# One graph-attention kernel: the queue orders of the last pair of heads are written out by hand

## The reference

```
h = relu(layernorm(x))
q = h @ wq.T + bq ; k, v likewise                    # 1024 x 1024 each
q2 = (q @ wiq.T + biq) as 16 heads of 64 ; k2, v2 likewise
mask = 384 x 384, -inf except at the 6,528 edges, where it is softplus(weight of the edge's type)
scores = q2 @ k2.T / 8 + mask ; attn = softmax(scores) ; o = attn @ v2   # for each head
out = x + (o of all heads, 384 x 1024) @ wo.T + bo
```

## Time and profile before

| | us |
|---|---|
| median of 3 runs | 301.51 |
| the runs | 300.0, 301.51, 301.77 |
| the profiled execution | 299.9 |
| its span, first to last instruction | 298.2 |
| PE busy | 286.0 |
| DVE, ACT, POOL busy | 179.3, 159.4, 153.4 |
| mean granted clock of PE | 0.994 |

### The profile page before, as it was taken

One profiled execution on the slowest core, in us unless ns is written; L12 is line 12 of the kernel. 1 busy time (PEld: TensorE's weight loads), 2 busy tenths in 40 slices (PEclk: granted clock), 3 DMA queues, 4 the chain that ended last, 5 costly groups with the idle time before them and its releaser, 6 DMA issues. The chain is left out here.

```text
span 298.2 us, 5957 instructions
## 1 busy us (share of the span) xinstructions
PE 286.0 (96%) x2325; PEld 266.7 (89%) x2325; DVE 179.3 (60%) x442; ACT 159.4 (53%) x287; POOL 153.4 (51%) x157
## 2 busy tenths in 40 slices
PE   6999999999999999999999899999999998959996
PEld 3799998888999999999999899999999995748885
DVE  4999778697576434444468665757666565372131
ACT  3886234362465223444345788778787879362000
POOL 6452445454465565554015959485674949660000
PEclk9999999999999999999999999999999999799999
DMA  7977865727634444344974234050421214200031
GB/s 264 326 248 269 311 212 189 228 75 261 244 129 143 141 143 141 96 116 113 261 178 106 63 82 120 25 141 20 126 73 70 86 61 141 73 0 2 0 141 70
DMA packets 16078, 40.90 MB, mean 137 GB/s; under 512 B 3737, under 2 KB 5170, under 8 KB 16050
## 3 DMA queue, kind: packets, MB, share of 16 engines
q1 hardware_dynamic: 13602, 38.53, 40.9%
q0 software_dynamic: 2016, 1.21, 1.8%
q10 hardware_dynamic: 432, 0.79, 0.7%
HBM read 37.71 MB, written 2.81 MB: 136 GB/s over the span
## 5 line engine op out<-in xcount | busy, mean ns | idle before, releaser
L483 POOL DMA_INDIRECT cells<-value,cell x51 | 55.3, 1085 | 56.2 <-DMA cells<-value,cell 40.5
L530 ACT ACTIVATE w_hi<-raw 128x1024 fp32r<-128x1024 f32 x50 | 51.7, 1054 | 22.8 <-PE banks L947 19.1
L945 PE MATMUL banks<-a_hi,w_hi 128*128 128x384 f32 x184 | 61.5, 334 | 0.0
L947 PE MATMUL banks<-a_lo,w_hi 128*128 128x384 f32 x184 | 61.5, 334 | 0.0
L946 PE MATMUL banks<-a_hi,w_lo 128*128 128x384 f32 x184 | 61.5, 334 | 0.0
L456 POOL TENSOR_TENSOR w_lo<-raw,w_hi 128x1024 fp32r<-128x1024 f32 x15 | 36.0, 2406 | 37.8 <-ACT w_hi L530 37.8
L817 DVE TENSOR_TENSOR w_lo<-raw,w_hi 128x1024 fp32r<-128x1024 f32 x35 | 42.3, 1229 | 9.9 <-ACT w_hi L530 9.8
L945 PEld LDWEIGHTS banks<-a_hi,w_hi 128*128 128x128 f32 x184 | 34.5, 188 | 0.1
L946 PEld LDWEIGHTS banks<-a_hi,w_lo 128*128 128x128 f32 x184 | 34.5, 188 | 0.0
L947 PEld LDWEIGHTS banks<-a_lo,w_hi 128*128 128x128 f32 x184 | 34.5, 188 | 0.0
L642 ACT ACTIVATE prob<-prob,neg_max 128x384 f32<-128x384 f32 x48 | 29.1, 607 | 9.1 <-DVE neg_max L877 9.0
(11 more groups left out here) (146 smaller groups left out, 600.3 us busy)
## 6 DMA issues: line engine op xcount, KB each, us to landing
raw<-in_slabs SPq DMA_DIRECT2D x40, 512.0 KB, 3.6
raw<-in_slabs SPq DMA_DIRECT2D x32, 256.0 KB, 3.9
prob<-key_rows SPq DMA_DIRECT2D x8, 256.0 KB, 4.2
x_sb<-in_x SPq DMA_DIRECT2D x3, 512.0 KB, 5.9
out_y<-x_sb SPq DMA_DIRECT2D x5, 256.0 KB, 2.1
cells<-prob SPq DMA_DIRECT2D x2, 576.0 KB, 7.6
cells<-value,cell POOLq DMA_INDIRECT x51, 3.4
x_sb<-in_x ACTq DMA_DIRECT2D x3, 256.0 KB, 4.2
```

The lines of the kernel that those rows point to most:

```text
L483: nc.gpsimd.indirect_dma_start(out=cells[c][:, :], out_offset=bass.IndirectOffsetOnAxis(ap=cell[:, t:t + 1], axis=0), in_=value[:, t:t + 1 ...
L530: nc.scalar.activation(split_place(s)[0], raw_place(s), ACT.Copy).then_inc(slab_hi, 1)
L945: nc.tensor.matmul(psum, w[0], a[0], start=first, stop=False)
L947: return nc.tensor.matmul(psum, w[0], a[1], start=False, stop=last)
```

## The change

On ACT, DVE and POOL the loop over pairs ends one pair earlier, and the last pair gets its own list. On ACT the exponentials of pair 7 and the `pt_hi` parts of pair 6 go ahead of the splitting of slabs 51 to 55. On DVE `head_part(5)` goes behind two maxima of pair 7, and the `pt_lo` and `head_part` calls of pairs 6 and 7 are dealt anew. On POOL the scaling of pair 7 comes ahead of all five slabs, with `pair_lo_part(5)` inside it. On PE the output products between the attention steps of the last pair are grouped anew: block 5 of pieces 0 and 1 joins one visit, and block 6 of pieces 0, 1 and 2 goes behind `pair_values(7)`. Away from the last pair there are two edits: on PE four of the 48 steps of pair 2 go ahead of `scores(1, 0)`, and on DVE `y_part(2)` goes behind the two `tile_lo_part` of pair 1.

```diff
--- before.py
+++ after.py
@@ -66,8 +66,9 @@
 LO_ALL = QK0 + 2 + AHEAD
 
 
-SLABS_OF_STEP = [((37 + 2 * j,), (38 + 2 * j,)) for j in range(PAIRS - 1)] + [((51, 52), (53,)), ((54, 55), ())]
-assert [s for step in SLABS_OF_STEP for part in step for s in part] == list(range(LO_ALL, SLABS))
+SLABS_OF_STEP = [((37 + 2 * j,), (38 + 2 * j,)) for j in range(PAIRS - 1)]
+LAST_SLABS = [51, 52, 53, 54, 55]
+assert [s for step in SLABS_OF_STEP for part in step for s in part] + LAST_SLABS == list(range(LO_ALL, SLABS))
 
 
 def tiles_of(group):
@@ -509,17 +510,24 @@
                     nc.gpsimd.tensor_scalar(prob_chunk(j, n, x), prob_chunk(j, n, x),
                                             row_inv[:, j % 2, c:c + 1], 1.0, ALU.mult, ALU.mult).then_inc(prob_ok, 1)
 
-            for j in range(PAIRS + 1):
+            for j in range(PAIRS - 1):
                 first, second = SLABS_OF_STEP[j]
-                if 2 <= j < PAIRS:
+                if j >= 2:
                     pair_lo_part(j - 2)
                 for s in first:
                     split_lo(s)
-                if j < PAIRS:
-                    for n in range(NT):
-                        norm_part(j, n)
+                for n in range(NT):
+                    norm_part(j, n)
                 for s in second:
                     split_lo(s)
+
+            last = PAIRS - 1
+            norm_part(last, 0)
+            norm_part(last, 1)
+            pair_lo_part(last - 2)
+            norm_part(last, 2)
+            for s in LAST_SLABS:
+                split_lo(s)
 
         @block.scalar
         def _(act):
@@ -661,30 +669,43 @@
                     nc.scalar.activation(half_sum[own, :], head_bank[x][other, 0:N], ACT.Identity,
                                          bias=bias[own, b:b + 1]).then_inc(half_ok, 1)
 
-            for j in range(PAIRS + 1):
+            for j in range(PAIRS - 1):
                 first, second = SLABS_OF_STEP[j]
-                if 2 <= j < PAIRS:
+                if j >= 2:
                     pair_hi_part(j - 2)
                 for s in first:
                     split_hi(s)
-                if j < PAIRS:
-                    for n in range(NT):
-                        exp_part(j, n)
+                for n in range(NT):
+                    exp_part(j, n)
                 if j >= 1:
-                    for m in range(2):
+                    for m in range(NT):
                         pt_hi_part(j - 1, m)
-                if j == PAIRS:
-                    pair_hi_part(PAIRS - 2)
-                if j >= 1:
-                    pt_hi_part(j - 1, 2)
-                if j < PAIRS - 1:
-                    for second_of in range(2):
-                        tile_hi_part(3 * KT + 2 * (j + 1) + second_of)
+                for second_of in range(2):
+                    tile_hi_part(3 * KT + 2 * (j + 1) + second_of)
                 for s in second:
                     split_hi(s)
                 if j >= 1:
                     half_part(j - 1)
-            pair_hi_part(PAIRS - 1)
+
+            last = PAIRS - 1
+            exp_part(last, 0)
+            exp_part(last, 1)
+            pt_hi_part(last - 1, 0)
+            pair_hi_part(last - 2)
+            exp_part(last, 2)
+            pt_hi_part(last - 1, 1)
+            pt_hi_part(last - 1, 2)
+            for s in LAST_SLABS[0:3]:
+                split_hi(s)
+            pt_hi_part(last, 0)
+            pt_hi_part(last, 1)
+            half_part(last - 1)
+            pt_hi_part(last, 2)
+            pair_hi_part(last - 1)
+            split_hi(LAST_SLABS[3])
+            half_part(last)
+            pair_hi_part(last)
+            split_hi(LAST_SLABS[4])
 
         @block.vector
         def _(dve):
@@ -906,33 +927,45 @@
                 dve.wait_ge(y_in, 16 * (NT + 1))
                 nc.vector.tensor_tensor(y[:, t, :], y[:, t, :], bo_sb, ALU.add).then_inc(y_ok, 1)
 
-            for j in range(PAIRS + 1):
-                if j < PAIRS:
-                    max_part(j, 0)
-                    if j == 0:
-                        y_part(0)
-                    max_part(j, 1)
-                    inv_part(j, 0)
-                    if j == 0:
-                        y_part(1)
-                    max_part(j, 2)
-                    inv_part(j, 1)
-                    if j == 0:
-                        y_part(2)
-                    inv_part(j, 2)
+            for j in range(PAIRS - 1):
+                max_part(j, 0)
+                if j == 0:
+                    y_part(0)
+                max_part(j, 1)
+                inv_part(j, 0)
+                if j == 0:
+                    y_part(1)
+                max_part(j, 2)
+                inv_part(j, 1)
+                inv_part(j, 2)
                 if j >= 1:
-                    for m in range(2):
+                    for m in range(NT):
                         pt_lo_part(j - 1, m)
-                if j == PAIRS:
-                    pair_lo_part(PAIRS - 2)
-                if j >= 1:
-                    pt_lo_part(j - 1, 2)
-                if j < PAIRS - 1:
-                    for second_of in range(2):
-                        tile_lo_part(3 * KT + 2 * (j + 1) + second_of)
-                if j >= 1:
+                for second_of in range(2):
+                    tile_lo_part(3 * KT + 2 * (j + 1) + second_of)
+                if j == 0:
+                    y_part(2)
+                if 1 <= j < PAIRS - 2:
                     head_part(j - 1)
-            pair_lo_part(PAIRS - 1)
+
+            last = PAIRS - 1
+            max_part(last, 0)
+            max_part(last, 1)
+            inv_part(last, 0)
+            head_part(last - 2)
+            inv_part(last, 1)
+            max_part(last, 2)
+            pt_lo_part(last - 1, 0)
+            inv_part(last, 2)
+            pt_lo_part(last - 1, 1)
+            pt_lo_part(last - 1, 2)
+            pt_lo_part(last, 0)
+            pt_lo_part(last, 1)
+            head_part(last - 1)
+            pt_lo_part(last, 2)
+            pair_lo_part(last - 1)
+            head_part(last)
+            pair_lo_part(last)
             dve.wait_ge(y_ok, NT)
             for i, (_, n, cols_out, psum) in enumerate(out_pieces):
                 dve.wait_ge(out_done, i + 1)
@@ -1153,12 +1186,12 @@
             pair_steps(1, 30, 40)
             scores(0, 2)
             pair_steps(1, 40, 48)
-            pair_steps(2, 0, 8)
+            pair_steps(2, 0, 12)
             for j in range(1, PAIRS - 1):
                 scores(j, 0)
-                pair_steps(j + 1, 8, 16)
+                pair_steps(j + 1, 12 if j == 1 else 8, 18 if j == 1 else 16)
                 scores(j, 1)
-                pair_steps(j + 1, 16, 24)
+                pair_steps(j + 1, 18 if j == 1 else 16, 24)
                 scores(j, 2)
                 pair_steps(j + 1, 24, 32)
                 turn(j - 1, 0)
@@ -1186,16 +1219,14 @@
             pair_values(last - 1)
             turn(last, 0)
             turn(last, 1)
-            out_part(1, range(3, 5))
-            for n in range(2):
-                out_part(n, range(5, 6))
+            out_part(1, range(3, 6))
+            out_part(0, [5])
             turn(last, 2)
-            for n in range(2):
-                out_part(n, range(6, 7))
             pair_values(last)
 
-
-            out_part(2, range(0, 7))
+            out_part(2, range(0, 6))
+            for n in range(3):
+                out_part(n, [6])
             out_part(3, range(0, 7))
             for piece in range(4):
                 out_part(piece, [KT - 1])
```

## The result

| | before | changed |
|---|---|---|
| median, us | 300.75 (299.73 to 301.77, 4 runs) | 291.99 (291.85 to 292.20, 4 runs) |
| ratio to before, 95% interval | | 0.9709 (0.9668 to 0.9751) |
| profiled execution, us | 299.9 | 291.85 |
| its span; mean granted clock | 298.2; 0.994 | 290.1; 1.0 |

The prediction was 293.0, range 291.0 to 296.8. Against the profiled execution the sum gave 292.1; it measured 291.85.

What follows compares the result with a forecast made beforehand. PE bounds the kernel, busy 286.0 of 298.2 us; tail 7.1 plus pair 1 0.7 makes 7.8 less: 292.1 from the profiled execution, 293.7 from the median. Taken between: 293.0, range 291.0 to 296.8.

Steps and rivals of the forecast that it cites:

- The tail, forecast 7.1: Last two pairs on PE: reordered queues remove three stalls and the fall of the clock, 7.1 us less.
- the 7.2 of the walk: Tail followed queue by queue to the product visit after `pair_values(7)`: 271.63 - 263.1 - 1.37, 7.2 us less.
- the sum by parts: Same tail gain: idle 5.48, later start 0.3, clock 1.4, one visit fewer 0.2, less a 0.3 wait: 7.1 us.
- The new wait, forecast 0.3: At `pair_values(7)` PE would wait 0.3 us for `head_part(6)` on DVE; `pt_lo(7,2)` had 0.2 to spare.
- the rival built on them: At `pair_values(7)`, a slip of one `half` and `head` (1.18 + 1.16) goes straight to PE: 295.3 us; chance 0.10.
- What I costed at nothing: Tail: moved `head_part(5)`, `pair_lo(6)`, later slabs and `norm(7,2)` would all be ready before PE wants them, 0 us.
- Pair 1, forecast 0.7: At `scores(1,0)`, four steps of pair 2 put ahead fill 0.7 of the 0.87 us wait: 0.7 us less.
- The clock, forecast 1.4: Tail from 255.74 to 260.02: PE ran below full clock, 4.28 us against 2.87; 1.4 us to be gained.
- The first rival: Tail: the clock falls all the same, 1.4 to 3 us of the gain lost, 295.4 us; chance 0.12.
- Slab supply: Last five slabs split some six us later; a slip of nine us loses 5: 298.5 to 300 us; chance 0.05.
- A long stretch at 1.2 GHz: Denser tail stays at the lower clock from `pair_values(6)` on; over 45 products 11 us lost, 304.5; chance 0.03.

Runs made afterwards that it cites:

- act_slabs_first: Changed kernel with ACT's old order up to the transposes of pair 6, and `head_part(5)` ahead of the first maximum on DVE: 296.47 us.
- pe_old: Changed kernel with PE's old order of output products in the last pair: 294.30 us, 0.9796 of the kernel before.
- pool_old: Changed kernel with POOL's old order, slabs 51 and 52 split ahead of the scaling of pair 7: 300.42 us, 0.9983 of the kernel before.
- tail_only: Changed kernel with the two edits of pair 1 taken back: 292.54 us, 0.9725 of the kernel before.
- fill_first: Kernel before with 13 useless matmuls on PE in the stall ahead of `turn(6,2)` alone: 300.57 us, 0.9985 of the kernel before.
- fill_last: Kernel before with useless matmuls on PE only in the stalls ahead of `turn(7,2)` and the output products of block 6: 299.96 us.
- fill_all: Kernel before with useless matmuls on PE in all three stalls of the tail, no wait removed: 298.77 us, 0.9929 of the kernel before.
- pool_only: Kernel before with POOL's new order alone: 301.23 us, 1.0006 of the kernel before.
- steps13: Changed kernel with 13 instead of 12 steps of pair 2 ahead of `scores(1,0)`: 291.57 us, 0.9682 of the kernel before.

## Why the prediction was right

**The bound.** PE's order of work was the bound, and its stalls, those of the tail above all, with the clock behind them were the prize: right. `act_slabs_first`, `pe_old` and `pool_old` bring 3.0, 2.4 and 6.5 us of idling back, and their fastest executions lie 3.15, 2.0 and 7.8 us above the changed kernel. The last pays for the clock too, which no execution of it kept.

**The tail, forecast 7.1.** Between `scores(7,0)` and equal work in the dense end the two traces differ by 7.4: 271.63 less 244.40 against 262.19 + 1.37 less 243.72 is 27.23 to 19.84. (The 1.37 are the six products that the change put behind this point.) In the kernel before `scores(7,0)` starts here:

```profile
244.40 0.44 PE L1091 MATMUL banks<-k_hi,q_hi 64*128 64x384 f32 x2
```

The 0.3 more is in small things: 0.1 up to `turn(6,1)`, which I had taken as unmoved; 0.15 since 24 transposes back to back take 0.89 and not twice 0.52; and the 7.2 of the walk that I had rounded down to the sum by parts. The 7.4 hold the clock's 1.4 too.

**The new wait, forecast 0.3.** It came, in two parts that the list of waits shows only on PE's weight loads (PEld, 240 to 264 us of the changed kernel):

```profile
PEld banks L1162 <- DVE pt_lo L912: 0.2, 1, 0.2
PEld banks L1162 <- DVE spare L922: 0.2, 1, 0.2
```

`pair_values(7)` starts 0.62 after `turn(7,2)` instead of 0.52, for `head_part(6)` (it writes `spare`), and takes 2.49 instead of 2.31, with 0.44 and 0.54 between its last groups, for `pt_lo(7,2)`. The two places I named as nearly late are those; the rival built on them cost 0.28 and no more.

**What I costed at nothing** cost nothing: `head_part(5)`, `pair_lo(6)`, the slabs, `norm(7,2)`. For `pair_lo(6)` between 0.6 and 2.4 us had been allowed; it took 0.55 because POOL was between two splits, which was a matter of where the two queues happened to stand. At 265.90 in the kernel before it took 1.77 beside one, and ended 0.4 behind it. In pair 1 the overlap fell the other way: DVE's add started 0.40 ahead of the split, overlapped it by 0.8 us, and POOL's two splits were 0.66 us longer (5.43 to 4.77). The Trainium skill, "SBUF — State Buffer", "SBUF: two separate sides", says that whichever of the two starts first keeps the shared ports for its whole instruction; both cases agree.

**Pair 1, forecast 0.7.** PE starts `scores(7,0)` 0.68 us earlier in the trace; the time shows 0.55 (`tail_only` against the changed kernel). That 7.8 came within 0.3 of the profiled executions (299.9 less 291.85 is 8.05) is partly luck: the tail gave 0.3 more and pair 1, by the time, 0.15 less.

**The clock, forecast 1.4: the term that was too small.** For the profiled execution the 1.4 were right. What was mis-sized is its share of the median: "one fall of the clock (1.4)" was taken to stand in every execution and a second one to explain the spread, with the gain put halfway between the two. I had one profiled execution of the kernel before, and it was of the milder group. 40 of 62 lose twice as much. An execution without any loss would take about 298.4 (298.43 and 298.44, the ones at 1.0 of `fill_first` and `fill_last`), so the clock costs the kernel before 1.5 us in one group (299.9) and 3.0 in the other (301.4); against the median of `fill_all`, 298.77, it is 1.1 and 2.6. Hence the median fell by about 9 us (300.75 and 301.27 to 291.99), and 7.8 were forecast against the profiled execution; the value between that I chose, 293.0, was one us too high, for I took the clock's share of the spread as halfway gained when it was gained in full.

**The first rival, that the mix of transposes and half-array products lowers the clock,** is refuted as the whole reason: the changed kernel and `tail_only` have that mix in the same places with no stall, and keep the clock in 14 of 14 executions; `fill_all`, which has every wait of the kernel before with full-array matmuls in it, in 6 of 6. I had argued for it from the second group of stalls, after which no fall followed in the profiled execution. `fill_first` has a clock below 1 in 11 of 12, and its trace shows the fall there. A single execution can't show that idling is harmless. The Trainium skill, "TensorE: Matmul & The Clock Gate", "What's actually happening", has the lower clock as the resting state that activity lifts; by it alone less idling could only help. `fill_all` against the kernel before agrees, and so does the changed kernel; across places the length of the stall does not decide, since 2.23 us in `fill_last` came with a fall in 12 of 13 executions and 2.44 in `pe_old` in 1 of 4.

**The other rivals.** Slab supply: `pool_only` and the changed kernel have the late slabs, and PE waits for none of them in either trace. A long stretch at 1.2 GHz: the lowest mean clock of nine executions of the changed kernel is 0.999. (Its price of 11 us on the chosen 293.0 gives 304.0, and not the 304.5 of the prediction.)

## What to carry to other kernels

When PE is full until the last stage, walk the tail queue by queue and ask of each item that stands ahead of a critical one when it is needed itself: two slab splits, 2 us on ACT and 4.8 on POOL, went behind the attention work at no cost. Queue orders of several engines can pay only together: one of them alone (`pool_only`) gained nothing, and without it (`pool_old`) the gain was gone; leaving out PE's (`pe_old`) cost only 2.3 us of it. To an idle time of two us or more on PE add what a fall of the clock behind it costs; here that was 1.3 to 3.0 us, in most executions though not in all.

## What the runs showed of the hardware that I had not expected

The same program has executions of different clock: `fill_first` spans 298.43 to 302.34 with mean clocks of 1.0, 0.994 and 0.989. With the stall of 2.23 us ahead of `turn(6,2)` one traced execution kept the clock (`fill_last`) and another lost it (the kernel before). A stall of 2.44 us (`pe_old`) lowered the clock in one of four executions, one of 2.23 (`fill_last`) in 12 of 13, two of 1.31 and 1.96 with 12 transposes between them (`fill_first`) in 11 of 12; one of 6.51 (`pool_old`) in ten of ten. Why 2.44 us in one place is milder than 2.23 in another stays open. Kernels without a stall beyond 0.9 us past 100 us (`tail_only`, `steps13`, the changed one twice) kept it in all 20 executions.
